# Centering destination rows in the TensorE accumulation of a graph network's last edge stage

## What is computed

```python
h = jnp.maximum(_layernorm(x, axis=-1), 0.0)
x = x + _L0_gnn_ref(h, src, dst, ...)      # four attention layers, 4 heads
h = jnp.maximum(_layernorm(x, axis=-1), 0.0)
x = x + _L1_gnn_ref(h, edge_attr_64, src, dst, ...)
...
total = jnp.concatenate([atom_src, atom_dst, nbr_fea], axis=1)   # 64 + 64 + 64
total = batch_norm(total @ W_full + b_full, bn1_g, bn1_b)        # 128 columns
filter_fea, core_fea = jnp.split(total, 2, axis=1)
nbr_msg = jax.nn.sigmoid(filter_fea) * jax.nn.softplus(core_fea)
atom_update = jax.ops.segment_sum(nbr_msg, edge_dst, num_segments=atom_in_fea.shape[0])
return jax.nn.softplus(atom_in_fea + batch_norm(atom_update, bn2_g, bn2_b))
```

## Time and profile before

| | |
|---|---|
| median of 3 runs | 3240.72 us (3231.77 to 3241.50) |
| the profiled execution | 3232.58 us, its span 3230.8 us |
| VectorE busy | 2235.8 us, 69% |
| TensorE busy (matmul) | 2319.8 us, 72% |
| GpSimd busy | 1427.3 us, 44% |
| ScalarE busy | 1248.5 us, 39% |
| mean granted clock of TensorE | 0.818 |

### The profile page before, as it was taken

One profiled execution on the slowest core, in us unless ns is written; L12 is line 12 of the kernel. 1 busy time (PEld: TensorE's weight loads), 2 busy tenths in 40 slices (PEclk: granted clock), 3 DMA queues, 4 the chain that ended last, 5 costly groups with the idle time before them and its releaser, 6 DMA issues. The chain is left out here.

```text
span 3230.8 us, 38240 instructions
## 1 busy us (share of the span) xinstructions
PE 2319.8 (72%) x10796; PEld 1499.2 (46%) x10796; DVE 2235.8 (69%) x3888; ACT 1248.5 (39%) x2599; POOL 1427.3 (44%) x1389
## 2 busy tenths in 40 slices
PE   1998888399788689889859977739977772110575
PEld 1766665255565445466635533325533331000565
DVE  4766664677777677677767744458889986664698
ACT  0333323244333234333324411114445556663587
POOL 5777774000677200377500067720057763777000
PEclk9999999999767689866759965559989985555898
DMA  2333332011444301255411111102233321222464
GB/s 60 105 108 99 94 100 78 15 46 46 101 124 123 85 32 46 62 124 125 118 30 47 46 37 34 34 13 79 78 74 72 72 63 30 63 71 67 138 202 139
DMA packets 310382, 248.80 MB, mean 77 GB/s; under 512 B 149840, under 2 KB 258639, under 8 KB 310154
## 3 DMA queue, kind: packets, MB, share of 16 engines
q1 hardware_dynamic: 266270, 197.56, 20.1%
q0 software_dynamic: 43904, 48.80, 8.3%
HBM read 125.76 MB, written 118.06 MB: 75 GB/s over the span
## 5 line engine op out<-in xcount | busy, mean ns | idle before, releaser
L930 POOL DMA_INDIRECT edge<-table,row_of_source x588 | 589.3, 1002 | 963.6 <-POOLq L753 778.8
L871 PE MATMUL banks<-scaled_t,w_heads 128*64 128x512 f32 x784 | 380.3, 607 | 0.0
L815 DVE TENSOR_TENSOR_SCAN wide<-keep,wide,banks 64x512 f32<-64x512 uint8 x196 | 249.5, 1273 | 187.4 <-issue 162.6
L1238 POOL DMA_INDIRECT edge<-table,row_of_x x196 | 227.3, 1160 | 303.4 <-POOLq L131 242.2
L981 PEld LDWEIGHTS banks<-w_edge_full,wide 128*128 128x128 f32 x1176 | 219.9, 279 | 146.6 <-issue 139.5
L849 ACT ACTIVATE ring<-wide 128x512 f32<-128x512 f32 x196 | 123.6, 630 | 425.1 <-DVE wide L815 425.1
L981 PE MATMUL banks<-w_edge_full,wide 128*128 128x72 f32 x1176 | 227.5, 360 | 70.5 <-DVE self_logit L1032 69.7
L1497 POOL DMA_INDIRECT node_rows<-rows_conv,scatter_row x196 | 218.9, 1117 | 118.3 <-ACT rows_conv L1535 68.0
L878 PEld LDWEIGHTS banks<-w_row,ring 128*128 128x128 f32 x1568 | 189.7, 191 | 160.9 <-issue 149.3
L974 PE MATMUL banks<-wide,w_row 128*64 128x512 f32 x294 | 250.6, 953 | 16.2 <-DVEq L1009 9.9
L1079 ACT ACTIVATE wide<-h_new 64x512 f32<-64x512 f32 x147 | 92.6, 630 | 435.4 <-DVE h_new L1022 435.4
(11 more groups left out here) (300 smaller groups left out, 4530.6 us busy)
## 6 DMA issues: line engine op xcount, KB each, us to landing
node_rows<-x_out SPq DMA_DIRECT2D x97, 256.0 KB
wide<-node_rows SPq DMA_DIRECT2D x48, 512.0 KB, 3.6
table<-chain_rows SPq DMA_DIRECT2D x147, 136.0 KB, 2.2
table<-rows SPq DMA_DIRECT2D x147, 136.0 KB, 2.3
nodes<-in_x_dram SPq DMA_DIRECT2D x97, 128.0 KB, 2.9
table<-x_out SPq DMA_DIRECT2D x97, 128.0 KB
out_dram<-n_soft SPq DMA_DIRECT2D x48, 256.0 KB, 2.1
sources<-src_pad SPq DMA_DIRECT2D x49, 196.0 KB
```

What stands on the lines that cost most here:

```text
L815: v.tensor_tensor_scan(out=wide[0:D, bass.ds(g * GE + 1, GE)], data0=keep[:, s], data1=bank[2 + s][0:D], initial=wide[0:D, bass.ds(g * GE, ...
L871: last = t_.matmul(bank[2 + s][0:D], w_heads[:, l, pair], scaled_t[:, s, pair], start=pair == 0, stop=pair == 1)
L930: pool.indirect_dma_start(out=edge[:, at_tile], out_offset=None, in_=tables[l], in_offset=bass.IndirectOffsetOnAxis(ap=row_of_source[:, at ...
L1238: pool.indirect_dma_start(out=edge[:, tile, 0:D], out_offset=None, in_=tables[l], in_offset=bass.IndirectOffsetOnAxis(ap=row_of_x1[:, tile ...
```

## The change

Four edits belong together.

1. **Destination rows centered on TensorE.** The first stage already has x of the destinations centered. SP now stores these rows too, as `x_mid` (`save_mid`), before `normalize` overwrites them, so `normalize` waits for the store. In the last edge stage SP loads x_mid where it loaded x_dst. TensorE adds them into bank 2 by a product with the identity, and multiplies h_full by `center_of`, identity less 1/64, in the same accumulation. Bank 2 then has the centered x1 of the destinations.
2. **VectorE's `center` keeps the source rows only** (a sum and a centering). ScalarE copies bank 2 into `norm` (`take_mid`), ahead of its squares.
3. **Edge attributes in pairs.** Two tiles of 64 features are transposed at once, so two transposes and a copy of 128x256 replace four and 64x512. The weights `w_conv3` stand twice, each time with zeros for the other tile of the pair, and the product is two of 256 columns where it was one of 512.
4. **x1 from the message table.** `edge` no longer has x1 of the destinations, so `load_x1` of the convolution stage reads the second part of the table in DRAM.

```diff
     x_dst = dram("x_dst", [P, TILES * D])
+    x_mid = dram("x_mid", [P, TILES * D])
...
-        w_conv3 = mem(top, "w_conv3", [D, 2 * D])
+        w_conv3 = mem(top, "w_conv3", [P, 2, 2 * D])
...
-                sp.dma_start(w_conv3[:], W_full[P:P + D]).then_inc(weights_loaded, 16)
+                for n, r in enumerate((0, D)):
+                    sp.dma_start(w_conv3[r:r + D, n], W_full[P:P + D]).then_inc(weights_loaded, 16)
...
+                v.memset(w_conv3[D:P, 0], 0.0)
+                v.memset(w_conv3[0:D, 1], 0.0)
...
+                def save_mid(k, g, s, turn):
+                    sp.wait_ge(centered, at(k))
+                    sp.sem_inc(sp_paced, 1)
+                    sp.dma_start(x_mid.rearrange("p (t f) -> p t f", f=D)[:, bass.ds(k * TPG, TPG)], norm[:, s % 2, :, 1]).then_inc(mid_saved[s % 2], 16)
...
-                pipelined(sp, ((1, save_x), (4, save), (0, load)), slots=SLOTS)
+                pipelined(sp, ((2, save_mid), (1, save_x), (4, save), (0, load)), slots=SLOTS)
...
                     v.wait_ge(rstd, at(k))
+                    v.wait_ge(mid_saved[h], 16 * (k // 2 + 1))
...
                 def load_x(k, g, s, turn):
-                    sp.wait_ge(x_used, at(k, back=2))
+                    sp.wait_ge(full_t, at(k, back=2))
                     sp.sem_inc(sp_paced, 1)
-                    sp.dma_start(x_again[:, s], x_dst.rearrange("p (t f) -> p t f", f=D)[:, bass.ds(g * TPG, TPG)]).then_inc(x_in[s], 16)
+                    sp.dma_start(x_again[:, s], x_mid.rearrange("p (t f) -> p t f", f=D)[:, bass.ds(g * TPG, TPG)]).then_inc(x_in[s], 16)
...
                 def to_edges(k, g, s, turn):
+                    t_.wait_ge(x_in[s], turn * 16 + 16)
+                    t_.wait_ge(mid_taken, at(k, back=1))
+                    t_.sem_inc(pe_paced, 1)
+                    t_.matmul(bank[2][:, 0:TPG * D], ident[:], x_again[:, s].rearrange("p t f -> p (t f)"), start=True, stop=False)
                     t_.wait_ge(full_ready, at(k))
-                    t_.wait_ge(x_used, at(k, back=1))
-                    t_.sem_inc(pe_paced, 1)
                     for t in range(TPG):
-                        last = t_.transpose(bank[2][:, t * D:(t + 1) * D], h_full[:, s, t * P:(t + 1) * P], ident[0:D, 0:D])
+                        last = t_.matmul(bank[2][:, t * D:(t + 1) * D], h_full[:, s, t * P:(t + 1) * P], center_of[:], start=False, stop=t == TPG - 1)
                     last.then_inc(full_t, 1)
...
-                    for t in range(TPG):
-                        last = t_.transpose(bank[3][0:D, t * P:(t + 1) * P], attr[:, s, t], ident[:])
+                    for a in range(2):
+                        last = t_.transpose(bank[3][:, a * P:(a + 1) * P], attr[:, s, 2 * a:2 * a + 2].rearrange("p t f -> p (t f)"), ident[:])
...
-                    t_.matmul(bank[5 + s][:], w_conv3[:], attr_t[:], start=False, stop=True).then_inc(conv_ready, 1)
+                    for b in range(2):
+                        last = t_.matmul(bank[5 + s].rearrange("p (a b q) -> p b a q", b=2, q=P)[:, b], w_conv3[:, b], attr_t[:],
+                                         start=False, stop=b == 1)
+                    last.then_inc(conv_ready, 1)
...
+                v.tensor_scalar(center_of[:], ident[0:D, 0:D], -1.0 / D, None, ALU.add).then_inc(center_set, 1)
...
                 def center(k, g, s, turn):
...
-                    link(v.tensor_reduce(now[:, 0, :, 0], here, AX_X, ALU.add))
-                    link(v.scalar_tensor_tensor(out=norm[:, s, :, 0], in0=inner(now[:, 0, :, 0], [P, TPG, D]), scalar=-1.0 / D,
-                                                in1=here, op0=ALU.mult, op1=ALU.add))
-                    v.wait_ge(x_in[s], turn * 16 + 16)
-                    v.wait_ge(full_t, at(k))
-
-                    v.tensor_tensor(here, bank[2][:, 0:TPG * D].rearrange("p (t f) -> p t f", f=D), x_again[:, s], ALU.add).then_inc(x_used, 1)
-                    v.wait_ge(x_used, at(k))
-                    v.sem_inc(sp_paced, 1)
-                    link(v.tensor_reduce(now[:, 0, :, 1], here, AX_X, ALU.add))
-                    assert count[0] == OWN
-                    v.scalar_tensor_tensor(out=norm[:, s, :, 1], in0=inner(now[:, 0, :, 1], [P, TPG, D]), scalar=-1.0 / D,
+                    v.tensor_reduce(total, here, AX_X, ALU.add).then_inc(own, 1)
+                    v.wait_ge(own, k + 1)
+                    v.scalar_tensor_tensor(out=norm[:, s, :, 0], in0=inner(total, [P, TPG, D]), scalar=-1.0 / D,
                                            in1=here, op0=ALU.mult, op1=ALU.add).then_inc(centered, 1)
...
+                def take_mid(k, g, s, turn):
+                    s_.wait_ge(full_t, at(k))
+                    s_.wait_ge(norm_in_psum, at(k, back=2))
+                    s_.activation(norm[:, s, :, 1], bank[2][:, 0:TPG * D].rearrange("p (t f) -> p t f", f=D), ACT.Copy).then_inc(mid_taken, 1)
+
                 def squares(k, g, s, turn):
+                    s_.wait_ge(mid_taken, at(k))
                     s_.wait_ge(centered, at(k))
...
-                    s_.activation(attr_t[:], bank[3][0:D], ACT.Copy).then_inc(norm_t_ready, 1)
+                    s_.activation(attr_t[:], bank[3][:, 0:2 * P], ACT.Copy).then_inc(norm_t_ready, 1)
...
-                pipelined(s_, ((1, finish), (4, rstd), (3, squares), (5, take), (6, keep_conv)), down=True, lead=LEAD)
+                pipelined(s_, ((1, finish), (4, rstd), (3, take_mid), (3, squares), (5, take), (6, keep_conv)), down=True, lead=LEAD)
...
-                    sp.dma_start(rows[:, s, :, 0:D], edge[:, bass.ds(g * TPG, TPG), 0:D]).then_inc(x1_in[s], 16)
+                    sp.dma_start(rows[:, s, :, 0:D],
+                                 tables[L - 1][N:N + EP].rearrange("(p t) w -> p t w", p=P)[:, bass.ds(g * TPG, TPG)]).then_inc(x1_in[s], 16)
```

More of the change, by code:

```diff
@@ L229, in build @@
             block = st.enter_context(nc.Block())
-            WEIGHT_LOADS = 2 * (L + H + 1) + 2 + 2 + 3 + 2
+            WEIGHT_LOADS = 2 * (L + H + 1) + 2 + 3 + 3 + 2
             ROWS_CONVERTED, KEEP_READY, INDICES_READY, WEIGHTS_SUMMED = 1, 2, 18, 46
@@ L421, in build @@
             x_saved = [sem(st, f"x_saved{s}") for s in range(SLOTS)]
+            mid_saved = [sem(st, f"mid_saved{n}") for n in range(2)]
             sources_in = sem(st, "sources_in")
@@ L1203, in build @@
             attr = mem(st, "attr", [P, 2, TPG, D])
-            attr_t = mem(st, "attr_t", [D, GE])
+            attr_t = mem(st, "attr_t", [P, 2 * P])
+            center_of = mem(st, "center_of", [D, D])
             stat = mem(st, "stat_last", [P, 2, 4, 2 * TPG])
@@ L1213, in build @@
             through, ended_ready, spread_out, full_ready, full_t, centered, squared, summed2, rstd_ready, \
-                norm_ready, norm_in_psum, attr_in_psum, norm_t_ready, conv_ready, conv_kept, conv_counted, x_used = [
+                norm_ready, norm_in_psum, attr_in_psum, norm_t_ready, conv_ready, conv_kept, conv_counted, mid_taken = [
                     sem(st, f"{name}_last") for name in (
@@ L1217, in build @@
                         "summed2", "rstd_ready", "norm_ready", "norm_in_psum", "attr_in_psum", "norm_t_ready",
-                        "conv_ready", "conv_kept", "conv_counted", "x_used")]
+                        "conv_ready", "conv_kept", "conv_counted", "mid_taken")]
+            center_set = sem(st, "center_set")
             own = sem(st, "own_last")
@@ L1274, in _ @@
                     t_.sem_inc(signal, AHEAD)
+                t_.wait_ge(center_set, 1)
                 def weights(k, g, s, turn):
@@ L1312, in _ @@
             def _(v):
-                for signal in (ended_ready, spread_out, x_used, centered, summed2, norm_ready, conv_counted):
+                for signal in (ended_ready, spread_out, centered, summed2, norm_ready, conv_counted):
                     v.sem_inc(signal, AHEAD)
                 v.memset(h_new[:, 1, 0:1], 0.0).then_inc(sp_paced, 1)
+                v.tensor_scalar(center_of[:], ident[0:D, 0:D], -1.0 / D, None, ALU.add).then_inc(center_set, 1)
                 v.memset(attr[:], 0.0).then_inc(zeroed, 1)
-                OWN = 3
                 def end(k, g, s, turn):
@@ L1332, in center @@
                 def center(k, g, s, turn):
[L1333 to L1342, removed]
+                    here = edge[:, bass.ds(g * TPG, TPG), 0:D]
+                    total = stat[:, s].rearrange("p n (t e) -> p n t e", e=2)[:, 0, :, 0]
                     v.wait_ge(gathered[s], turn * (16 * TPG) + 16 * TPG)
@@ L1376, in _ @@
                 pipelined(v, ((5, normalize), (1, end), (1, back), (4, variance), (3, center), (7, count_in)), down=True, lead=LEAD)
-                count = [G * OWN]
+                count = [G]
                 def link(ins):
@@ L1398, in _ @@
                 s_.preload_act_table_set(ACT_TABLES)
-                for signal in (full_ready, squared, rstd_ready, norm_t_ready, conv_kept):
```

(1 more changed line is left out.)

## The result

The changed kernel takes 3204.93 us (median of 4 runs, 3201.53 to 3218.61) against 3236.24 for the kernel before on the same chip (4 runs, 3229.40 to 3241.50): a ratio of 0.9914, interval 0.9893 to 0.9934. Forecast were 3197 us and a range of 3177 to 3225. The time is inside; the profile shows that one step behind it was wrong all the same.

A forecast was written before the change was run, and what follows sets the result against it. VectorE and GpSimd share the 5.95 us round; GpSimd binds after. Stage 319 to 272.6 us (245 gathers, 4 + 2 locks, 2 tie, 1.6 landing, 18 end), less 2 elsewhere: 44 saved, 3188.6, plus 8.1 gives 3197; range 3177 to 3225.

The forecast's parts named there:

- VectorE falls to 4.47 us a round: Last edge stage: three VectorE instructions go and L1347 to L1374 shortens, so the round drops from 5.95 by 1.48 us.
- GpSimd becomes the bound: Last edge stage: four unchanged gathers, 0.94 + 0.30 us each, take 4.99 us a group, more than VectorE's 4.47.
- What of the locks stays: Gathers held by two-SBUF-input VectorE instructions: mostly gone in a steady 5.05 us round; 4 + 2 us left over the stage.
- the locks stay: Rival: rows landing later than 1.55 us put the scan over the next first gather; 5.54 per group, 3216 us; chance 0.10.
- TensorE's sum, 5.04, a tie: Last edge stage: TensorE's work per group rises from 4.1 to 5.04 us, tying with GpSimd's 5.05; 2 us over the stage.
- TensorE becomes the bound: Rival: at a clock of 0.93 TensorE's round is 5.4 us, 13 us less saved, 3210 us; chance 0.14.
- Transposes of h made into products: TensorE: four transposes of h become eight matmuls, +0.66 us a group; kept as transposes, some 2 us less over the stage.
- The end of the stage: Last landing to L1386: 30.5 us now, about 3.5 rounds after; 22 us at 1.2 GHz, 13 at 2.4, taken as 18.
- First stage: 49 added stores of 128 KB and a wait for them cost 0 to 2 us, taken as 1.5; setup 0.5.
- The other side: Rival: TensorE stays at 1.2 GHz, its round some 9.8 us, the stage grows by 170 us, 3410 us; chance 0.04.
- the first two rivals with half of each other: High end of the range, 3225 us: TensorE as bound (3210) and the locks staying (3216), each with half the other.
- 5.05 to 5.15 apart: Confirming sign in the last edge stage: the distance in us between successive VectorE scans.

The follow-up runs named there:

- after_scan_psum: Changed kernel with segment ends written back into their PSUM bank, so the last edge stage's scan has one input in SBUF: 3185.63 us, ratio 0.9849.
- after_psum_no_h: after_scan_psum without the eight products of h with center_of: 3176.44 us, ratio 0.9854.
- after: The changed kernel with all four edits, first set of runs, against the kernel before: 3204.93 us, ratio 0.9914.
- after_again: The changed kernel with no further edit, run again for a second profile: 3206.50 us over 9 runs, ratio 0.9924.
- after_no_h: Changed kernel without the eight matmuls of h_full by center_of: 3219.17 us, ratio 0.9957.
- before_pairs: Kernel before with the third edit alone, edge attributes transposed two tiles at a time: 3224.24 us, ratio 0.9976.
- after_both_psum: after_scan_psum plus, in the convolution stage, exponential and message written to PSUM banks, the scan reading from there: 3163.46 us, ratio 0.9792.
- after_psum_fours: after_scan_psum with the third edit undone, attributes transposed in four and one product of 512 columns: 3200.93 us, ratio 0.9921.
- before_scan_psum: Kernel before with segment ends written back into PSUM, so the scan has one input in SBUF: 3236.65 us, ratio 1.0004.

## Why the prediction held, point by point, and where it did not

- **VectorE falls to 4.47 us a round.** Right: 4.63 in the rounds in which it waits for nothing.
- **GpSimd becomes the bound, 196 x 1.25 = 245 us of gathers.** Right where nothing holds a gather: 247.3 in after_scan_psum, of which 2.06 are the pause. after_psum_no_h shows that it is the floor.
- **"What of the locks stays": 4 + 2 us.** This is the step that failed: a term of 6 us that measured 38 and 18. 196 x (1.141 - 0.945) is 38 us in the profile of after and 196 x (1.035 - 0.945) 18 in that of after_again. The working placed VectorE's instructions between gathers that start 1.25 us apart, found that placement to hold itself, and stopped. after_again has a placement like it, with the scan from 2454.14 to 2455.42 and the next gather at 2455.23 under its last 0.2, and there a gather takes 0.95. But it isn't the only one that holds itself, and the working gave VectorE no second one: a round of 4.63 and one of 7.00. The rival "the locks stay" had the mechanism (rows landing late, the scan over a gather) and was priced as one steady round of 5.54; the mean of the alternation is 5.83, and its condition was met by the group before, not by a later landing throughout.
- **TensorE's sum, 5.04, a tie.** Right in size: 5.00 measured, clock 1.00. Its terms were off both ways and nearly cancelled: the attribute product was taken as unchanged at 0.95 and is 0.86, w_conv the same, while weights, identity and transposes take 1.01, 0.53 and 0.71 for 0.95, 0.48 and 0.68. "TensorE becomes the bound", 3210, did not come: after_no_h has less of its work and no shorter rounds.
- **Transposes of h made into products.** The Trainium skill (Perfetto Trace Analysis, section Transposes) asks for a transpose where one is meant, not a standard matmul. The price of not doing so was put at 2 us over the stage. In after_psum_no_h all eight products are gone and the stage isn't shorter, so no run here shows a price.
- **The end of the stage, 18 us, range 13 to 22.** Right in size, 16.7 and 15.2. The forecast put it between the two clock levels. It came out at the higher level, 0.86 in the window above, and before_pairs shows the attribute pairs alone to be enough for that: 13 us of drain in its profile. That is a third of what the stage wins in the profile of after_again and most of what it wins in that of after, from the edit that the prediction costed as two transposes and a shorter copy.
- **First stage, 1.5 us; setup; x1 from the table.** Hidden, all three: the first stage's last gather of source rows at 531.1 and 531.0, the store's landing at 3.7 us within the 3 to 4 forecast, the convolution stage 272.8 and 273.1 us.
- **The other side, TensorE at 1.2 GHz, 3410.** Did not come. The clock is 0.98 or more in every window from 2400 to 2600 of the changed kernel that was read.

The time of 3205 thus comes from a stage that is 17 us shorter in one execution and 39 in another, where 46 were forecast. The number came close in part by luck. The runs mix the two patterns, the better one has the forecast's pace, and how many fall into which stood in no working. And the forecast counts 8.1 us for the distance of the median of three runs from the profiled one; 24 and 16 later runs of the kernel before have medians of 3234.79 and 3233.24, 1 to 2 us above it, so that without this term the forecast is some 3190. The high end, "the first two rivals with half of each other", is 3220 to 3223 by the prediction's own prices and not 3225, which changes nothing here. The pace "5.05 to 5.15 apart" and "gathers of 0.94 nearly throughout" are refuted by the profile of after and true for half of after_again. What starts the alternation early in the one execution (its seventh group) and only behind the pause in the other was not settled.

## What to carry to other kernels

When a change takes the bound from VectorE and a descriptor-writing GpSimd is next, a steady round that works on paper is not enough: lay two consecutive rounds side by side and ask whether a long and a short one also hold each other up. Cheaper than finding the right phase is to take the contact away: a two-input VectorE instruction that can read one operand from PSUM stops holding gathers, which gave nothing while VectorE was the bound (1.0004) and 17 to 40 us of the stage once it wasn't. And an edit to TensorE's shapes is to be priced by the products beside it too.

## What the runs showed that was not expected

- GpSimd stops for 1.55 to 3.79 us before the same gather, the 114th of this stage, in all twelve profiles, waiting for nothing that is recorded.
- Nine runs of after_again spread over 36 us (3192 to 3228), and runs of after_scan_psum and after_both_psum, without the holds, over 9 and 5 us (3180 to 3189, 3161 to 3166). That the two patterns make the spread is not shown: four runs of after_psum_no_h spread over 14 us, and 24 of the kernel before over 27.
- A landing takes 1.55 us after the gather's end, 2.3 when it is held to the end of the scan and SP's loads start with it, 1.9 when the larger of these is cut. Some take 2.8 to 3.2 without a scan over the gather.
- The attribute product of 512 columns takes 1.05 us through 64 rows and 0.86 through 128, in two pieces; the products on both sides of it gain 0.09 and 0.10.
- With the attributes in pairs TensorE stays near 2.4 GHz at the end of the stage (0.92), without them it was at 0.50; but it is at 1.00 in after_psum_fours, which has none, and in before_scan_psum, which has none either, it falls for good only in the last 15 us of the stage.
